# A Macaron transformer block on one core: the low halves of the expert weights are taken against a PSUM copy, the first shared results are summed by TensorE, and some table loads are issued later

## The chip, the cores and the metric

The kernel runs on one core of a Trainium2 chip. The metric is the device time of one execution in microseconds; the span of a profiled execution is the time from its first to its last instruction. TensorE is called PE here, its weight loads PEld, VectorE DVE, ScalarE ACT, GpSimd POOL and SyncE SP, as in the profile.

## What is computed

Two batches of 512 tokens with 256 features go through a mixture-of-experts layer, an attention layer and the same mixture-of-experts layer again, each added to the residual. The change lies in the first of the three.

```python
x = x + 0.5 * ffn(layernorm(x))          # 16 experts of width 128, 2 per token, and one shared expert
x = x + attention(layernorm(x))
x = x + 0.5 * ffn(layernorm(x))

def ffn(xt):
    probs = softmax(xt @ Wr.T + bias);  val, idx = top_k(probs, 2);  w = val / (val.sum() + 1e-9)
    y = (silu(xt @ Wg[e]) * (xt @ Wu[e])) @ Wd[e]          # for each expert e
    routed = sum over the two chosen experts of w * y
    shared = (silu(xt @ sWg) * (xt @ sWu)) @ sWd
    return routed + shared
```

## The kernel before

All products are taken in a three-term form: each fp32 operand is split into a high half that TensorE's one-pass format (`F32R`) holds exactly and a low half, the remainder, and `three` sums high times high, high times low and low times high. So each expert's weights, 768 words on each of 128 partitions, need a split: ACT copies `w_raw` to `wh` in the format of the high half (`split_high`, L656), and DVE subtracts `wh` from `w_raw` to get `wl` (`split_low`, L1230). `wl` lies on the memory of `w_raw`. Expert number q in the order of use is `order[q]`; q = 0 is the shared expert, 1 to 16 are the routed ones.

The engines run their own instruction lists in the order written and meet at semaphores; there is no scheduler. The first `ffn` has these stages:

- **Routing** (`route`): DVE works out for each token its two experts and the row (`slot`) of a table `slots_x` in DRAM that the token goes to. POOL then writes the normalised tokens there by 16 indirect DMAs (`scatter`, L565).
- **The shared expert** over eight tiles of 128 tokens, as a pipeline of turns i. In turn i PE runs `gate_up` of tile i (six matmuls of 256 columns), `hidden_turn` of tile i-1 (a transpose by the identity) and `down` of tile i-2 (three matmuls); ACT takes the silu of tile i (`sg`, L675), the high half of the hidden tile i-1 (`hT_h`, L681) and `split_high(8 + i)`; DVE multiplies (`hm`, L1330), takes the low half of the hidden tile (`hT_l`, L1334), adds half of the result of tile i-3 to the residual `res` (L1347) and runs `split_low`: one expert a turn up to turn 5, two a turn in turns 6 to 10.
- **The routed blocks**: 31 blocks of 128 rows of `slots_x`, loaded by SP as `xp` in pairs once all scatters have landed (L415), each through the same steps with the weights of its own expert. Before the first block PE waits for all low halves (`s_wlo_v`), for the residual sums (`s_ysh`), for the table of experts and for the scatters (`s_sc[3]`), and then runs six matmuls that only keep it busy (`keep_busy`, L877). The results go back to DRAM by one indirect DMA each (L576), from a ring of four buffers `ysb`.

SP loads the experts in order: ten together at the start, the last six in pairs, each pair behind a step of the scatters. Ahead of the ten, SP loads small tables for the attention mask (`place_k`, `place_q`, and `rows_k`, `rows_q` from `before` and `within`, which POOL fills). `s_place` counts POOL's four table steps.

## Time and profile before

| | us |
|---|---|
| median of three runs | 348.19 |
| lowest, highest | 347.44, 352.12 |
| the profiled execution | 348.41 |
| its span | 346.7 |
| shared expert, first matmul to the end of the last low half | 24.84 to 53.55 |
| first transpose of a routed block | 56.16 |

In the span PE is busy 74%, DVE 70%, ACT 48% and POOL 45% of the time. A row of the timeline gives the start in us, the duration in us, engine, line, operation and tiles, "x4" for four merged instructions, and in brackets the idle time before it and what ended that. A row of the chain of waits gives start, duration and the work. A row of the busy time by stretch gives the stretch, its length, the busy time of PE, PEld, DVE, ACT and POOL with their instructions, the granted PE clock as a share of 2.4 GHz, the share of the DMA engines and GB/s. A row of the groups gives line, engine, operation, tiles, shapes and count, then the busy time in all, the mean of one in ns, and the idle time before them.

### The profile page before, as it was taken

What the parts mean: (1) busy time and instruction counts of PE and PEld (TensorE: products, weight loads), DVE (VectorE), ACT (ScalarE), POOL (GpSimd) and SP (SyncE); (2) the same over time, 40 slices, a digit from 0 to 9 for tenths busy, and PEclk for the clock granted to TensorE, in tenths of its full rate; (3) what the DMA queues carried; (4) which work ended last, traced back from release to release, by engine and by line L of the source; (5) the groups of instructions that cost most, each with busy time, mean ns of one, the idle gap of its engine ahead of it and who ended that gap; (6) DMA issues with size and microseconds to landing.
All of it is one profiled execution on the core that took longest, in us unless ns stands there. A gap on an engine that the chain in (4) does not pass through costs nothing.

```text
span 346.7 us, 6303 instructions
## 1 busy us (share of the span) xinstructions
PE 255.0 (74%) x1812; PEld 185.4 (53%) x1815; DVE 243.5 (70%) x800; ACT 167.0 (48%) x433; POOL 155.6 (45%) x248
## 2 busy tenths in 40 slices
PE   1828537999991677987998999889459069999900
PEld 0528515999980255543343444457248039999800
DVE  8787593788876971758888889457586018888726
ACT  3486531555553155457656667773423015565400
POOL 7207770466766003303768733320027704776620
PEclk9967855999996899999999999999969769999955
DMA  7996919154512517991543300000002261456137
GB/s 252 407 363 207 352 66 298 45 149 122 177 53 70 174 47 195 229 285 60 126 93 94 94 2 3 1 3 0 0 20 104 106 197 50 148 159 189 30 110 253
DMA packets 30472, 46.23 MB, mean 133 GB/s; under 512 B 5391, under 2 KB 23573, under 8 KB 30056
## 3 DMA queue, kind: packets, MB, share of 16 engines
q1 hardware_dynamic: 24776, 33.97, 31.5%
q0 software_dynamic: 5664, 11.87, 11.0%
q8 instruction: 16, 0.26, 0.3%
q14 instruction: 16, 0.13, 0.1%
HBM read 27.98 MB, written 20.61 MB: 140 GB/s over the span
## 4 chain that ended last, share of the span: by engine, by line
PE 44%; DVE 22%; DMA 11%; POOL 8%; ACT 7%; issue 5%; SPq 1%; another core or an unknown queue 1%; POOLq 0%; DVEq 0%; ACTq 0%
PE bank L314 21%; POOL slots_x L565 5%; PE bank L1073 5%; DVE bank L1458 5%; PE bank L968 4%; PE bank L1036 3%; PE bank L321 3%; DVE wl L1230 3%; DMA results<-ysb,xp 2%; DMA yg<-results 2%; DMA w_raw<-in_experts 2%; DVE res L1402 2%; PE bank L892 2%; ACT ct L841 2%; DMA slots_x<-xn,slot 2%
## 5 line engine op out<-in xcount | busy, mean ns | idle before, releaser
L576 POOL DMA_INDIRECT results<-ysb,xp x62 | 60.9, 983 | 51.3 <-issue 35.0
L1458 DVE CUSTOM_DVE_ANT_0 bank<-bank,dec 128x512 f32<-128x512 f32 (+3 forms) x128 | 59.5, 520 | 14.9 <-PE bank L1036 13.6
L841 ACT ACTIVATE ct<-bank 128x512 f32<-128x512 f32 (+1 forms) x96 | 44.4, 521 | 19.6 <-PE bank L1049 19.2
L565 POOL DMA_INDIRECT slots_x<-xn,slot x32 | 33.5, 1048 | 33.1 <-DVE slot L1307 23.8
L622 POOL TENSOR_SCALAR_AFFINE_SELECT ct<-ct 128x256 f32<-128x256 f32 x64 | 24.5, 407 | 39.9 <-ACT ct L841 39.9
L721 ACT ACTIVATE xT_h<-bank 128x256 fp32r<-128x256 f32 x62 | 23.8, 384 | 38.4 <-PE bank L968 36.8
L314 PE MATMUL bank<-wh,xT_h 128*128 x124 | 40.9, 329 | 1.4 <-DVE xT_l L1357 1.2
L1330 DVE TENSOR_TENSOR hm<-sg,bank 128x128 f32<-128x128 f32 x78 | 22.4, 287 | 23.9 <-ACT sg L675 23.9
L1357 DVE TENSOR_TENSOR xT_l<-bank,xT_h 128x256 fp32r<-128x256 f32 x62 | 26.2, 423 | 18.5 <-ACT xT_h L721 18.3
L675 ACT ACTIVATE sg<-bank 128x128 f32<-128x128 f32 x78 | 21.5, 276 | 36.1 <-PE bank L314 36.0
L1036 PE MATMUL bank<-stk_q,stk_k 96*128 96x512 bf16 (+3 forms) x128 | 33.9, 304 | 3.0 <-DMA stk_q<-parts_d 1.3
L314 PE MATMUL bank<-wh,xT_l 128*128 x124 | 35.3, 285 | 0.0
L314 PE MATMUL bank<-wl,xT_h 128*128 x124 | 35.3, 284 | 0.0
L314 PE MATMUL bank<-wh,hT_h 128*128 (+1 forms) x78 | 29.7, 381 | 2.7 <-DVE res L1347 2.1
L1049 PE MATMUL bank<-stk_k,stk_q 120*128 120x512 bf16 (+3 forms) x128 | 30.1, 300 | 1.3 <-DMA stk_k<-mT 0.8
L877 PE MATMUL bank<-below_b,ident_b 128*128 128x512 bf16 x35 | 12.7, 513 | 22.1 <-DMA slots_x<-xn,slot 10.1
L1369 DVE COPY ysb<-bank 128x256 f32<-128x256 f32 x62 | 25.7, 415 | 2.4 <-DMA results<-ysb,xp 1.3
L892 PE MATMUL bank<-ident,hm 128*128 128x128 f32 x78 | 22.4, 287 | 6.4 <-DVE hm L1330 6.3
L314 PEld LDWEIGHTS bank<-wh,xT_h 128*128 128x128 f32 x124 | 23.9, 193 | 3.2 <-issue 3.1
L968 PE MATMUL bank<-ident,xp 128*128 128x128 f32 x124 | 24.7, 286 | 0.4 <-issue 0.4
L596 POOL DMA_DIRECT2D stk_q<-parts_d x24 | 12.2, 515 | 27.8 <-DMA parts_d<-part 20.9
L1036 PEld LDWEIGHTS bank<-stk_q,stk_k 96*128 96x128 bf16 x128 | 10.7, 97 | 25.3 <-DVE mmax L1458 19.6
(188 smaller groups left out, 671.0 us busy)
## 6 DMA issues: line engine op xcount, KB each, us to landing
xp<-slots_x SPq DMA_DIRECT2D x30, 257.0 KB, 2.8
w_raw<-in_experts SPq DMA_DIRECT2D x17, 384.0 KB, 6.3
yg<-results SPq DMA_DIRECT2D x16, 256.0 KB, 4.6
slots_x<-zeros SPq DMA_DIRECT2D x2, 1285.0 KB, 11.4
parts_d<-part SPq DMA_DIRECT2D x6, 384.0 KB, 3.9
stk_k<-parts_d SPq DMA_DIRECT2D x8, 192.0 KB, 3.8
stk_q<-parts_d POOLq DMA_DIRECT2D x8, 192.0 KB, 4.6
slots_x<-zeros SPq DMA_DIRECT2D x1, 1413.5 KB, 7.3
```

Of the source, the lines that this page charges most:

```text
L314: mm = eng.matmul(to, xs(k, a), ws(k, b), start=i == 0, stop=i == len(terms) - 1)
L565: pool.indirect_dma_start(slots_x, where, xn[:, t, :], None)\
L576: pool.indirect_dma_start(results, where, ysb[c % RING][:], None, bounds_check=4 * N - 1, oob_is_err=False).then_inc(s_ys[c % RING], 16)
L622: pool.affine_select(out=pair, in_=pair, compare_op=ALU.is_ge, fill=0.0, base=0, pattern=[[0, 2], [1, P]], channel_multiplier=-1).then_inc ...
L841: act.activation(ct[n % 6][:, a:b], bank[2 + i][:, 0:b - a], ACT.Exp).then_inc(s_exp, 1)
L892: pe.transpose(bank[4 + par][:, 0:P], hm[par][:], ident[:]).then_inc(s_ht, 1)
L968: mm = pe.transpose(bank[b % 2][:, k * P:(k + 1) * P], xb[b % XRING][:, k * P:(k + 1) * P], ident[:])
L1036: pe.matmul(bank[s_bank[num % 3]][:, 0:(i + 1) * P], stk_k[g % NSTK][0:STK, u, i * P:(i + 1) * P], stk_q[g % NSTK][0:STK, u, 0:(i + 1) * P ...
L1049: mm = pe.matmul(to[:, at:at + SEQ - j * P], q[:, u, j * P:(j + 1) * P], k[:, u, j * P:SEQ], start=at == 0, stop=True, skip_group_check=True)
L1357: dve.tensor_tensor(xT[b % 2][1][:], bank[b % 2][:, 0:D].rearrange("p (k t) -> p k t", k=KT), xT[b % 2][0][:].bitcast(F32), ALU.subtract). ...
L1369: dve.tensor_copy(ysb[r][:], bank[6 + (j - 3) % 2][:, 0:D]).then_inc(s_ye, 1)
L1458: dve.tensor_tensor_reduce(s_i, s_i, dec[:, SEQ - w:SEQ], 1.0, NEG, ALU.add, ALU.max, mmax[g % 2][:, n % G * QT + i:n % G * QT + i + 1])\
```

## The change

Four things are changed, all in the first `ffn` and ahead of it.

- `split_low_beside` takes the place of `split_low` for the 16 routed experts. PE multiplies the high half `wh` by an identity (`show_high`, two matmuls of 384 columns) into two PSUM banks, banks 6 and 7 for even q and 0 and 1 for odd q, and DVE subtracts these copies from `w_raw` in two instructions of 384 columns. `show_high(q)` waits for the high half and, since the banks are used again, for the low half of expert q-2.
- `down_and_add` takes the place of `down` for the shared tiles: PE adds twice the residual, by an fp32 matmul with a doubled identity, to the three products in PSUM banks 4 and 5, and ACT copies half of the sum to `res`. The addition on DVE is gone. Banks 4 and 5 also hold the transposed hidden tiles, so `hidden_turn` now waits for ACT's copy of the tile that was there.
- POOL fills the two identities (`ident_r`, `ident_2`) in the set-up. `iota_i` is made smaller.
- SP waits for two of POOL's table steps instead of four before the first mask tables, and loads `rows_k` and `rows_q` behind the first ten experts.

In PE's list, turn 3 of the shared expert (tile 3 enters, tile 2 is turned, tile 1 is brought down) ends like this before:

```order
L314 MATMUL bank<-wh,xnT_l 128x256
L892 MATMUL bank<-ident,hm 128x128 [waits s_htl,s_hm]
L314 MATMUL bank<-wh,hT_h 128x256 [waits s_htl]
L314 MATMUL bank<-wl,hT_h 128x256
L314 MATMUL bank<-wh,hT_l 128x256
L314 MATMUL bank<-wh,xnT_h 128x256 [waits s_hm]
```

and like this now, where L904 is the transpose, L914 and L916 are `down_and_add` and L958 is `show_high`:

```order
L319 MATMUL bank<-wh,xnT_l 128x256
L904 MATMUL bank<-ident,hm 128x128 [waits s_htl,s_hm,s_ysh]
L914 MATMUL bank<-res,ident 128x256 [waits s_htl]
L916 MATMUL bank<-wh,hT_h 128x256
L916 MATMUL bank<-wl,hT_h 128x256
L916 MATMUL bank<-wh,hT_l 128x256
L958 MATMUL bank<-wh,ident_r 128x384 [waits s_wlo_v,s_whi]
L958 MATMUL bank<-wh,ident_r 128x384
L319 MATMUL bank<-wh,xnT_h 128x256 [waits s_hm]
```

The transpose has a wait on ACT's copy (`s_ysh`) more, and the gate matmuls of the next tile stand behind two copies that wait for DVE (`s_wlo_v`).

In DVE's list, turn 8, where two experts are split and the last tiles come down, reads before:

```order
L1334 TENSOR_TENSOR hT_l<-bank,hT_h 128x128 [waits s_hth]
L1347 SCALAR_TENSOR_TENSOR res<-bank,res 128x256 [waits s_y]
L1230 TENSOR_TENSOR wl<-w_raw,wh 128x768 [waits s_whi] x2
```

and now, where L1282 is `split_low_beside` and L1387 the low half of the hidden tile:

```order
L1282 TENSOR_TENSOR wl<-w_raw,bank 128x384 [waits s_whp]
L1282 TENSOR_TENSOR wl<-w_raw,bank 128x384
L1282 TENSOR_TENSOR wl<-w_raw,bank 128x384 [waits s_whp]
L1282 TENSOR_TENSOR wl<-w_raw,bank 128x384
L1387 TENSOR_TENSOR hT_l<-bank,hT_h 128x128 [waits s_hth]
```

Each split now waits for PE's copy (`s_whp`), and the low half of the hidden tile has moved behind the splits of its turn.

The diff:

```diff
@@ -153,7 +153,9 @@
         oh = sb("oh", [P, 2, NT, E], F32, r2)
         ohs = sb("ohs", [P, NT, E], BF16, r2)
         big = sb("big", [P, NB * E], F32, r2)
-        iota_i = sb("iota_i", [P, 512], I32, r2)
+        iota_i = sb("iota_i", [P, 512 - 2 * P], I32, r2)
+        ident_r = sb("ident_r", [P, P], F32R, r2)
+        ident_2 = sb("ident_2", [P, P], F32, r2)
         mx = sb("mx", [P, NT], F32, r2)
         rsum = sb("rsum", [P, NT], F32, r2)
         top = sb("top", [P, 2, NT], F32, r2)
@@ -207,6 +209,7 @@
         s_w = [sem(f"s_w{q}") for q in range(E + 1)]
         s_whi = sem("s_whi")
         s_wlo_v = sem("s_wlo_v")
+        s_whp = sem("s_whp")
         s_rw = sem("s_rw")
         s_zero = sem("s_zero")
         s_eps = sem("s_eps")
@@ -295,6 +298,8 @@
 
         order = [E] + list(range(E))
         EARLY = 8
+        wh_bank = ((6, 7), (0, 1))
+        WP = WE // 2
         NJ = NT + NB
 
 
@@ -394,14 +399,15 @@
             sp.dma_start(ob[:], o_b.partition_broadcast(P)).then_inc(s_small, 16)
 
             at = SEQ + 1 + P
-            sp.wait_ge(s_place, 4)
+            sp.wait_ge(s_place, 2)
             for to in (place_k[0:3, :], place_q[5:8, :]):
                 sp.dma_start(to[0:2, :], masks[0:2, at:at + SEQ]).then_inc(s_msk, 16)
                 sp.dma_start(to[2:3, :], masks[6:7, at:at + SEQ]).then_inc(s_msk, 16)
+            for q in range(1, EARLY + 3):
+                load_expert(q)
+            sp.wait_ge(s_place, 4)
             sp.dma_start(rows_k[6:, :], before[:]).then_inc(s_msk, 16)
             sp.dma_start(rows_q[8:, :], within[:]).then_inc(s_msk, 16)
-            for q in range(1, EARLY + 3):
-                load_expert(q)
 
 
             for q, (gate_sem, count) in zip(range(EARLY + 3, E + 1, 2), ((s_to, 2), (s_sc[0], 8 * NT), (s_to, 3))):
@@ -534,6 +540,8 @@
             link(pool.memset(ones_b[:], 1.0))
             link(pool.affine_select(out=below_b[:], in_=ones_b[:], compare_op=ALU.is_gt, fill=0.0, base=0,
                                     pattern=[[1, P]], channel_multiplier=-1))
+            link(pool.tensor_copy(ident_r[:], ident[:]))
+            link(pool.tensor_scalar(ident_2[:], ident[:], 2.0, None, ALU.mult))
             pool.tensor_copy(ident_b[:], ident[:]).then_inc(s_const, 1)
             link(pool.memset(before[:], NEG))
             pool.affine_select(out=before[:], in_=before[:], compare_op=ALU.is_ge, fill=0.0, base=-1,
@@ -700,9 +708,13 @@
                 if f == 0:
                     for q in range(3, EARLY):
                         split_high(q)
-                for i in range(NT + 2):
+                for i in range(NT + 3):
                     if i < NT:
                         hidden(f * NJ + i, (f * NJ + i) % 2, i < 2 and not f)
+                    if f == 0 and 0 <= i - 3 < NT:
+                        act.wait_ge(s_y, i - 2)
+                        act.activation(res[:, i - 3, :], bank[4 + (i - 3) % 2][:, 0:D], ACT.Copy, scale=0.5)\
+                            .then_inc(s_ysh, 1)
                     if 0 <= i - 1 < NT:
                         hidden_high(f * NJ + i - 1, (f * NJ + i - 1) % 2, i - 1 < 2 and not f)
                     if f == 0 and EARLY + i <= E:
@@ -896,6 +908,14 @@
                 three(pe, bank[6 + par][:, 0:D], lambda k, a: hT[par][a][:], lambda k, b: wd(b),
                       [(0, 0, 0), (0, 0, 1), (0, 1, 0)]).then_inc(s_y, 1)
 
+            def down_and_add(t):
+                to = bank[4 + t % 2][:, 0:D]
+                pe.wait_ge(s_htl, t + 1)
+                pe.matmul(to, ident_2[:], res[:, t, :], start=True, stop=False)
+                for a, b in ((0, 0), (0, 1), (1, 0)):
+                    mm = pe.matmul(to, hT[t % 2][a][:], (wh, wl)[b][:, E, KT * GU:WE], start=False, stop=a == 1)
+                mm.then_inc(s_y, 1)
+
             def logits(n, r):
 
                 pe.wait_ge(s_tlo, number(n, r))
@@ -930,6 +950,19 @@
                     pe.wait_ge(s_wlo_v, 1)
                 pe.wait_ge(s_slot, 2 * f + 1)
 
+                def show_high(q):
+                    pe.wait_ge(s_whi, q + 1)
+                    if q > 2:
+                        pe.wait_ge(s_wlo_v, q - 1)
+                    for c in range(2):
+                        mm = pe.matmul(bank[wh_bank[q % 2][c]][:, 0:WP], ident_r[:],
+                                       wh[:, order[q], c * WP:(c + 1) * WP], start=True, stop=True,
+                                       skip_group_check=True)
+                    mm.then_inc(s_whp, 1)
+
+                if f == 0:
+                    show_high(1)
+
                 def w_s(k, b):
                     return (wh, wl)[b][:, E, k * GU:(k + 1) * GU]
 
@@ -938,11 +971,21 @@
                     if i < NT:
                         gate_up(j, j % 2, f == 0 and i < 2, rows(i), w_s)
                     if 0 <= i - 1 < NT:
+                        if f == 0 and i >= 3:
+                            pe.wait_ge(s_ysh, i - 2)
                         hidden_turn(j - 1, (j - 1) % 2, f == 0 and i - 1 < 2)
                     if 0 <= i - 2 < NT:
-                        if i - 2 >= 2:
+                        if f and i - 2 >= 2:
                             pe.wait_ge(s_ysh, f * NT + i - 3)
-                        down(j - 2, j % 2, lambda b: (wh, wl)[b][:, E, KT * GU:WE])
+                        if f == 0:
+                            down_and_add(i - 2)
+                        else:
+                            down(j - 2, j % 2, lambda b: (wh, wl)[b][:, E, KT * GU:WE])
+                    if f == 0:
+                        for q in (i + 2,) if i < 6 else (2 * i - 4, 2 * i - 3):
+                            show_high(q)
+                if f == 0:
+                    show_high(E)
                 pe.wait_ge(s_ysh, (f + 1) * NT)
                 if f == 0:
                     pe.wait_ge(s_wlo_v, E + 1)
@@ -1230,6 +1273,16 @@
                 dve.tensor_tensor(wl[:, e, :], w_raw[:, e, :], wh[:, e, :].bitcast(F32), ALU.subtract)\
                     .then_inc(s_wlo_v, 1)
 
+            def split_low_beside(q):
+                e = order[q]
+                for c in range(2):
+                    part = slice(c * WP, (c + 1) * WP)
+                    if c == 0:
+                        dve.wait_ge(s_whp, q)
+                    ins = dve.tensor_tensor(wl[:, e, part], w_raw[:, e, part], bank[wh_bank[q % 2][c]][:, 0:WP],
+                                            ALU.subtract)
+                ins.then_inc(s_wlo_v, 1)
+
             def statistics(r):
                 for t in (2 * r, 2 * r + 1):
                     ins = dve.bn_stats(stats[:, t, :], res[:, t, :])
@@ -1340,15 +1393,15 @@
                     j = f * NJ + i
                     if i < NT:
                         times_up(j, j % 2, f == 0 and i < 2)
+                    if f == 0:
+                        for q in (i + 1,) if i < 6 else (2 * i - 5, 2 * i - 4):
+                            split_low_beside(q)
                     if 0 <= i - 1 < NT:
                         hidden_low(j - 1, (j - 1) % 2)
-                    if 0 <= i - 3 < NT:
+                    if f and 0 <= i - 3 < NT:
                         dve.wait_ge(s_y, j - 2)
                         dve.scalar_tensor_tensor(out=res[:, i - 3, :], in0=bank[6 + (j - 3) % 2][:, 0:D], scalar=0.5,
                                                  in1=res[:, i - 3, :], op0=ALU.mult, op1=ALU.add).then_inc(s_ysh, 1)
-                    if f == 0:
-                        for q in (i + 1,) if i < 6 else (2 * i - 5, 2 * i - 4):
-                            split_low(q)
 
                 def step(b, live):
                     j = f * NJ + NT + b
```

## Rows read from the trace of the kernel before

**Rows 1.** Busy time by stretch, the shared expert.

```profile
24.80:30.70 5.90, 5.57 (x25) 5.30 (x26) 5.48 (x18) 5.68 (x12) 4.22 (x4) 0.50 0.79 306
...
40.90:44.35 3.45, 1.65 (x10) 1.05 (x9) 2.22 (x5) 2.97 (x7) 2.47 (x3) 0.99 0.63 244
44.35:53.65 9.30, 2.50 (x8) 1.64 (x8) 9.20 (x16) 2.04 (x4) 5.37 (x6) 0.50 0.31 97
```

**Rows 2.** The chain of waits in order of time, end of the shared expert.

```profile
45.08 0.33 DVE res L1347
...
51.81 1.75 DVE wl L1230 x2
...
53.65 2.72 PE bank L877 x6
```

**Rows 3.** Groups of DVE by shape, 18 to 112 us.

```profile
L1230 DVE TENSOR_TENSOR wl<-w_raw,wh 128x768 fp32r<-128x768 f32 x16 | 14.8, 947 | 0.0
L1357 DVE TENSOR_TENSOR xT_l<-bank,xT_h 128x256 fp32r<-128x256 f32 x31 | 13.1, 422 | 4.4 <-ACT xT_h L721 4.3
```

**Rows 4.** The timeline of PE, at half clock.

```profile
25.19 0.42 PE L314 MATMUL bank<-wl,xnT_h 128*128 128x256 f32 x1
25.41 0.41 PE L314 MATMUL bank<-wh,xnT_l 128*128 128x256 f32 x1
```

**Rows 5.** The same timeline, where the clock has risen.

```profile
30.44 0.39 PE L314 MATMUL bank<-wh,xnT_h 128*128 128x256 f32 x1
...
31.84 0.28 PE L314 MATMUL bank<-wl,xnT_h 128*128 128x256 f32 x1
31.96 0.28 PE L314 MATMUL bank<-wh,xnT_l 128*128 128x256 f32 x1
```

**Rows 6.** The same timeline in the attention: fp32 matmuls, four heads side by side.

```profile
166.47 1.07 PE L1073 MATMUL bank<-ct,V 128*32 128x512 f32 x8
...
169.55 0.64 PE L1073 MATMUL bank<-ct,V 128*32 128x256 f32 x8
```

**Rows 7.** The chain of waits among the blocks: two transposes.

```profile
71.69 0.22 PE bank L968 x2
```

**Rows 8.** The timeline of ACT, 35 to 42 us.

```profile
35.71 0.84 ACT L656 ACTIVATE wh<-w_raw 128x768 fp32r<-128x768 f32 x1 [3.81 <-DMA w_raw<-in_experts]
36.46 0.26 ACT L675 ACTIVATE sg<-bank 128x128 f32<-128x128 f32 x1
36.62 0.27 ACT L681 ACTIVATE hT_h<-bank 128x128 fp32r<-128x128 f32 x1
...
41.09 0.84 ACT L656 ACTIVATE wh<-w_raw 128x768 fp32r<-128x768 f32 x1 [3.13 <-DMA w_raw<-in_experts]
```

**Rows 9.** Groups of ACT by shape over the span.

```profile
L721 ACT ACTIVATE xT_h<-bank 128x256 fp32r<-128x256 f32 x62 | 23.8, 384 | 38.4 <-PE bank L968 36.8 <-issue 1.4
```

**Rows 10.** The timeline of POOL, set-up and scatters.

```profile
7.47 0.29 POOL L537 CAST ident_b<-ident 128x128 bf16<-128x128 f32 x1
...
13.21 0.19 POOL L557 COPY xn<-to_row 128x4 int32<-128x4 int32 x1 [2.23 <-DVE xn L1245]
...
43.03 1.62 POOL L565 DMA_INDIRECT slots_x<-xn,slot  x1 [0.52 <-POOL xn L557]
44.96 0.97 POOL L565 DMA_INDIRECT slots_x<-xn,slot  x1 [0.30 <-issue]
```

**Rows 11.** The timeline of SP's queue.

```profile
14.55 0.62 SPq L401 DMA_DIRECT2D rows_k<-before  x1
...
51.22 2.94 SPq L415 DMA_DIRECT2D xp<-slots_x  x6
```

**Rows 12.** DMA issues of the page, the blocks' loads: KB, us to landing.

```profile
xp<-slots_x SPq DMA_DIRECT2D x30, 257.0 KB, 2.8
```

**Rows 13.** Busy time by stretch: first transpose to first result, first and second expert layer.

```profile
56.16:63.21 7.05, 6.46 (x36) 5.99 (x35) 2.98 (x10) 2.79 (x10) 0.00 (x0) 0.63 0.62 214
...
282.22:287.85 5.63, 5.04 (x34) 4.26 (x35) 2.84 (x10) 2.54 (x9) 0.00 (x0) 0.91 0.62 195
```

## The prediction

> **What bounds the kernel now.** I read the chain of waits first, then the busy time by stretch, then the timelines of the engines in the first expert layer, since the diff touches nothing behind it. The chain shows that the shared expert ends on DVE: pairs of low halves of 1.73 to 1.75 us with a residual sum of 0.33 us between them, five times, up to 53.56; PE starts its six busy matmuls at 53.65 and the first block's transposes at 56.16 [rows 2, 13]. In that stretch PE is busy 2.50 of 9.30 us and DVE 9.20 [rows 1]. Two other things are close behind: ACT had waited 3.81 and 3.13 us for weights that landed at 35.71 and 41.09 [rows 8], and SP could load the blocks only from 51.22, when the last scatter had landed [rows 11]; a load lands 2.8 us after its issue [rows 12], so PE could not have begun a block before 54. The path that the change can shorten is thus worth about 2 us (56.16 to 54), plus what PE's clock gives: it is at 1.2 GHz from 44.35 on [rows 1], and from the first transpose to the first result the first layer takes 7.05 us at a mean clock of 0.63, the second layer, with the same work, 5.63 at 0.91 [rows 13].
>
> **The prices.** DVE: a low half of 768 columns takes 0.947, a subtraction of 256 columns with one operand in PSUM 0.422 [rows 3], that is 1.03 ns a column; so 384 columns take 0.55, and as the next may start 0.08 earlier (0.947 against half of 1.75), two hold DVE for 0.93, against 0.87 before. A PSUM operand costs nothing visible: the 256-column row lies on the same line. PE at 2.4 GHz: a matmul of 256 columns follows the last by 0.12 and ends 0.16 after that [rows 5]; at half clock by 0.21 to 0.22 [rows 4]. A copy (two of 384) is then 0.34, or 0.65 at half clock, and can be read 0.16 later, at 0.50. The fp32 matmul with the doubled identity has no twin in the trace. Below: two identity transposes of 128 columns take 0.22 [rows 7], above: the eight records of 256 columns of the attention take 0.64; I take the slope between its two rows, 1.07 less 0.64 for 256 columns more, 0.43 [rows 6], since that row, like this matmul, multiplies fp32 and doesn't only move it. The Trainium skill (FP8 and Floating Point Precision, section TensorE Precision Notes) says that a true fp32 product takes four passes through the array, which by the one-pass row would be an estimate of 0.47, far from the transposes' 0.22; with 0.22 the stage below ends 1.0 us earlier, and by the slope the trace agrees with the page. So the sum and product of one tile, `down_and_add`, is 0.43 + 3 x 0.12 = 0.79, against 0.36 before.
>
> **Part by part.** *Low halves beside a copy, and the residual on PE.* DVE alone would gain: in turns 6 to 10 ten splits cost 0.07 more each, five sums of 0.33 are gone, -0.95. But each turn of PE now has a ring of waits: gate matmuls until ACT can start its silu 0.95 (6 x 0.12, the tail, the semaphore), silu 0.16 [rows 8], ACT's copy of an earlier sum 0.42 (0.384 for 256 columns [rows 9] and the semaphore), for which the transpose waits, transpose 0.10, sum 0.79, copy 0.34, and only then the next gate matmuls: 2.76. The walk: PE is busy for 5.57 of the first 5.90 us at half clock [rows 1], so the three copies that stand ahead of the fourth gate group delay it by 3 x 0.65, from 30.44 [rows 5] to 32.4. From there the clock is full. Four turns of 2.76, 0.33 for the weights of 35.71, which ACT must still split ahead of a silu, and a second copy of 0.33 in turn 6 bring the gate matmuls of the last tile to 44.1. The weights of 41.09 are no longer waited for. The sum of tile 5 starts 1.63 later, at 45.7. Now PE and DVE hand over to each other: sum 0.79, copy 0.50, one split 0.93, low half of the hidden tile 0.33 (0.29 by the slope of rows 3, and the semaphore), then the next sum: 2.55, twice, to 50.8. The last time it is sum, copy, three splits and 0.16 to PE: 4.24. PE is let go at **55.1**, 1.4 us later than at 53.65. With the two bounds of the fp32 matmul it is 54.1 and 56.4.
>
> *Behind it.* If the clock is full there, the six busy matmuls take half of the 2.51 us from 53.65 to 56.16, 1.25: transposes at 56.3, +0.2. From there to the first result it is 5.63 instead of 7.05, -1.4. The sum is **-1.2 us**. After the first result the blocks run at full clock already, so the shift passes on to the end, through a list that isn't changed.
>
> *The scatters.* A scatter takes 0.97 when DVE reads PSUM or rests, and 1.62 where it starts beside low halves read from two SBUF operands [rows 10]; five of the 16 take 1.2 or more. The last scatter should land up to 2 us before 51.2, and the blocks be loaded before 52. With PE let go at 55.1 this is worth nothing; it is also why a scatter that isn't quickened costs nothing.
>
> *Tables later.* SP reaches the experts earlier by the two loads that now stand behind them, 0.62 us of issue for one [rows 11], and by the shorter wait. ACT may then split the first experts some 1.2 us earlier, but PE's first gate matmuls wait for DVE's routing, and the half-clock stretch above is PE's own: worth nothing to 0.3. `rows_k` and `rows_q` are read by ACT only after the last tile, long after they land. *POOL's two identities* take about 0.29 each like the cast beside them, and its next deadline, 13.21, has 2.23 us of idle time before it [rows 10]: nothing. *ACT's eight copies* of 0.38 lie in the ring, counted. Behind each waiting copy on PE stand the gate matmuls of the next tile, which ACT and DVE wait for; that is the ring too.
>
> **Rivals.** *The clock falls.* Between 40.90 and 44.35 PE was busy 1.65 of 3.45 us at full clock and fell to half at its end [rows 1]. In the ring it is busy 1.95 of 2.76 us (gate matmuls 0.72, transpose 0.10, sum 0.79, copy 0.34), but late, in the hand-over, 0.79 + 0.68 of 2.55, little more than the half of the stretch that fell. The Trainium skill (TensorE: Matmul & The Clock Gate, section What's actually happening) says that the throttled state is the default and activity releases it; by that rule more matmuls can only help, but the row at 40.90 shows a half-busy engine falling. If it falls near the end, the blocks start as cold as before: +1.4 from 55.1, 349.7. If a stretch of the ring runs at half clock as well, +1.1 on top and no gain behind it, 350.8; with all from 44 on at half clock PE is let go at 58.5, 353. This is the case that ends on the other side, decided by whether PE's gaps after 44 us pull the clock down. *The ring isn't there.* If the waits overlap better than I walked them, DVE sets the end as the change says: 53.65 less 0.95 is 52.7, busy matmuls at full clock to 53.95, blocks loaded by then: -2.2, and -1.4 behind: 344.8. For it: at full clock a copy of 0.50 fits into a split of 0.93. Against: the low half of the hidden tile now stands behind two splits, and the sum, and with it the copy, behind that. *Half clock throughout.* With the ring at 1.2 GHz the walk ends beyond 61, +8 or more, 356; PE would be busy nearly without a gap then, and in the first 5.90 us that raised the clock [rows 1]. *It does not do what it says*, scatters or loads keep their times: same time as the forecast, since neither is late.
>
> **How the numbers follow.** The profiled execution took 348.41, the median of the three is 348.19, 0.2 less; 348.41 less 1.2 is 347.2, from the median 347.0, and I say 347.1. Chances: forecast with the clock held 0.55 (346.0 to 348.5 with the bounds of the fp32 matmul), clock falls 0.23 (349.7 to 353), ring not there 0.18 (344.3 to 345.5), half clock throughout 0.04. The range takes in the forecast, half of the ring's absence and the falling clock up to one cold stretch: 344.6 to 351.0. Two per cent, about what a measurement of this kernel can tell from no change, is 7 us: only half clock throughout reaches it, and part of the falling clock could with bad luck; nothing here is worth 7 us of gain. Faster 0.01, same 0.94, slower 0.05.
>
> **What the profile after would show.** Right: DVE idle for some 0.5 us ahead of splits with PE's copy as releaser; PE waiting for ACT's `res` in turns 3 to 7; scatters all near 0.97; the six busy matmuls starting 1 to 2 us later than 53.65 with their waits last on DVE, and taking about 1.25 us. Wrong: DVE without gaps from 42 us on, a fp32 record pair away from 0.43, or a granted clock of 0.5 after 44 us.

## The result, and the profile after

The changed kernel takes 352.21 us (median of 20 runs, 348.25 to 356.85), the kernel before, timed beside it, 348.78 (345.01 to 352.12). The ratio is 1.0075, with a 95% interval of 1.0048 to 1.0102. That is 2.6 us by the ratio and 3.4 by the medians (the medians hold all runs, the ratio leaves out those more than 1.5% above the fastest): slower, though by less than 2%. The prediction was 347.1, with a range that ended at 351.0. The profiled execution took 352.48, with a span of 350.7.

PE's timeline in turn 6 of the shared expert and at the start of turn 7, after (start, duration, engine, line, work, and in brackets the idle time ahead and what ended it):

```profile
41.56 0.28 PE L319 MATMUL bank<-wh,xnT_h 128*128 128x256 f32 x1
...
43.07 0.33 PE L904 MATMUL bank<-ident,hm 128*128 128x128 f32 x1 [0.64 <-ACT res L716]
43.24 0.60 PE L914 MATMUL bank<-res,ident 128*128 128x256 f32 x2
...
44.03 0.87 PE L958 MATMUL bank<-wh,ident_r 128*128 128x384 f32 x4
44.73 0.29 PE L319 MATMUL bank<-wh,xnT_h 128*128 128x256 f32 x1
```

and ACT's in turn 6:

```profile
42.46 0.28 ACT L683 ACTIVATE sg<-bank 128x128 f32<-128x128 f32 x1 [0.83 <-PE bank L319]
42.64 0.38 ACT L716 ACTIVATE res<-bank 128x256 f32<-128x256 f32 x1
```

This is the ring, step by step: gate matmuls at 41.56, silu 0.90 later, ACT's copy 0.18 behind it, the transpose 0.43 behind that with `res` of ACT as its releaser, the sum from 43.24 to 44.03 (0.79), the copies of the high halves, and only then the next gate matmuls. A turn with one copy takes 2.82 us (33.11, 35.93, 38.75, 41.56). From 44 us on DVE waits for PE's copies:

```profile
44.58 1.02 DVE L1282 TENSOR_TENSOR wl<-w_raw,bank 128x384 fp32r<-128x384 f32 x2 [0.59 <-PE bank L958]
...
47.77 1.02 DVE L1282 TENSOR_TENSOR wl<-w_raw,bank 128x384 fp32r<-128x384 f32 x2 [0.59 <-PE bank L958]
...
53.19 2.88 DVE L1282 TENSOR_TENSOR wl<-w_raw,bank 128x384 fp32r<-128x384 f32 x6 [0.57 <-PE bank L958]
```

PE's end of the stage, after, and the busy time by stretch (columns as in [rows 1]):

```profile
54.36 0.59 PE L958 MATMUL bank<-wh,ident_r 128*128 128x384 f32 x2 [0.85 <-DVE wl L1282]
56.17 1.76 PE L889 MATMUL bank<-below_b,ident_b 128*128 128x512 bf16 x6 [1.22 <-issue]
57.72 0.63 PE L1011 MATMUL bank<-ident,xp 128*128 128x128 f32 x2
```

```profile
24.80:30.70 5.90, 4.82 (x21) 4.71 (x22) 5.07 (x19) 4.87 (x10) 3.22 (x3) 0.57 0.71 272
44.35:53.65 9.30, 6.80 (x39) 5.41 (x37) 7.19 (x17) 4.14 (x12) 2.98 (x5) 1.00 0.54 163
...
57.72:65.17 7.45, 6.86 (x36) 6.46 (x35) 2.90 (x10) 2.78 (x10) 0.00 (x0) 0.58 0.10 38
```

In the stretch 44.35 to 53.65, at a granted clock of 0.50 before [rows 1], the clock is 1.00. PE is let go at 56.17, where it was 53.65 before [rows 2]. The six busy matmuls take 1.55 to the first transpose instead of 2.51, but then the clock falls: from the first transpose to the first result it is 7.45 us at a mean clock of 0.58, where 5.63 was expected [rows 13].

The scatters did what the prediction said: all but the first take 0.96 to 0.98, where 1.62 stood before [rows 10], and SP loads the blocks from 49.08 instead of 51.22 [rows 11]. PE doesn't wait for that.

```profile
46.56 0.96 POOL L573 DMA_INDIRECT slots_x<-xn,slot  x1 [0.30 <-issue]
```

```profile
49.08 2.94 SPq L421 DMA_DIRECT2D xp<-slots_x  x6
```

In these two profiles the first layer accounts for 1.3 us (last result of a block copied at 106.39, before at 105.09), and 2.8 are lost behind it, in code that the change doesn't touch. Whether that second part belongs to the change was the first thing to settle.

### The profile page after: what moved, and what is told of

Read it like the earlier page. It is cut to its first block, busy times and chain, and to the rows that moved or that the text cites. A ratio compares the mean times of both kernels' runs of the same rounds, so it can differ in the third digit from the quotient of the medians.

```text
span 350.7 us, 6428 instructions
## 1 busy us (share of the span) xinstructions
PE 265.0 (76%) x1863; PEld 194.6 (55%) x1863; DVE 243.0 (69%) x808; ACT 170.7 (49%) x441; POOL 153.2 (44%) x250
## 4 chain that ended last, share of the span: by engine, by line
PE 43%; DVE 19%; POOL 10%; DMA 10%; issue 10%; ACT 7%; SPq 1%; POOLq 0%; DVEq 0%
PE bank L319 17%; PE bank L1116 5%; DVE bank L1511 5%; POOL slots_x L573 4%; DMA results<-ysb,xp 4%; PE bank L326 3%; PE bank L1079 3%; POOL results L584 3%; PE bank L1011 3%; DMA yg<-results 2%; ACT ct L853 2%; PE bank L904 2%; DVE res L1455 2%; PE bank L1092 2%; PE bank L958 2%
## 5 line engine op out<-in xcount | busy, mean ns | idle before, releaser
L573 POOL DMA_INDIRECT slots_x<-xn,slot x32 | 31.4, 982 | 33.5 <-DVE slot L1360 24.5
L319 PE MATMUL bank<-wh,xT_h 128*128 x124 | 41.9, 338 | 2.0 <-DVE xT_l L1410 2.0
L319 PEld LDWEIGHTS bank<-wh,xT_h 128*128 128x128 f32 x124 | 24.9, 201 | 3.4 <-issue 3.3
L319 PE MATMUL bank<-wh,hT_h 128*128 (+1 forms) x70 | 25.7, 367 | 0.9 <-DVE hT_l L1387 0.4
L904 PE MATMUL bank<-ident,hm 128*128 128x128 f32 x78 | 22.2, 285 | 4.0 <-ACT res L716 3.2
L319 PEld LDWEIGHTS bank<-wl,xT_h 128*128 128x128 f32 x124 | 25.1, 202 | 0.0
L319 PEld LDWEIGHTS bank<-wh,xT_l 128*128 128x128 f32 x124 | 24.8, 200 | 0.0
```

The costliest lines, as they stand in the source:

```text
L319: mm = eng.matmul(to, xs(k, a), ws(k, b), start=i == 0, stop=i == len(terms) - 1)
L573: pool.indirect_dma_start(slots_x, where, xn[:, t, :], None)\
L904: pe.transpose(bank[4 + par][:, 0:P], hm[par][:], ident[:]).then_inc(s_ht, 1)
```

## Experiments

The theories. **The ring** (of waits on PE, with ACT's copy in it) lets PE go late. **The cold tail**: the clock falls while PE waits from 53 to 56, and the blocks start at half clock. **The set-up**: POOL's two identities delay the routing. **Luck**: what is lost behind the first layer is a matter of single executions. The medians and ratios, each against the kernel before timed beside it (20 runs of the changed kernel, 6 of ident_act, 12 of each other):

| kernel | median | before | ratio, 95% |
|---|---|---|---|
| changed | 352.21 | 348.78 | 1.0075 (1.0048 to 1.0102) |
| copy_first | 349.88 | 347.78 | 1.0059 (1.0026 to 1.0092) |
| no_copies | 351.15 | 347.78 | 1.0091 (1.0055 to 1.0128) |
| no_sum | 350.61 | 347.78 | 1.0060 (1.0026 to 1.0094) |
| ident_act | 354.27 | 347.78 | 1.0107 (1.0024 to 1.0189) |
| setup_only | 348.69 | 348.41 | 1.0030 (0.9991 to 1.0070) |
| before_busy | 347.62 | 348.41 | 0.9991 (0.9946 to 1.0036) |
| after_busy | 350.21 | 348.41 | 1.0059 (1.0024 to 1.0095) |
| best1 | 347.16 | 348.41 | 0.9980 (0.9942 to 1.0018) |
| before_fill | 347.05 | 348.89 | 0.9941 (0.9911 to 0.9971) |
| after_fill | 351.33 | 348.89 | 1.0051 (1.0014 to 1.0087) |
| before_all | 345.03 | 348.89 | 0.9880 (0.9843 to 0.9917) |
| best2 | 345.91 | 348.89 | 0.9946 (0.9906 to 0.9986) |

### The ring: copy_first

```diff
                 for i in range(NT + 3):
-                    if i < NT: hidden(...)
                     if f == 0 and 0 <= i - 3 < NT: ... res[:, i - 3, :] copied
+                    if i < NT: hidden(...)
```

> The changed kernel, with ACT's residual copy of a turn ahead of its silu instead of behind it. If the ring of waits sets the end of the shared expert, a turn of PE in turns 4 to 7 falls from 2.82 to about 2.4 us, PE no longer waits 0.64 us for ACT's res, and the six busy matmuls start at about 54.9 instead of 56.17; the last result scatter of the first layer then comes about 1.2 us earlier and the median falls by as much, 0.3%. If DVE's splits alone set the end, the busy matmuls still start at 56.0 to 56.3 and the time stays. If the cold start behind it is what costs, the block transposes come earlier but the gate matmuls behind them still run at half clock, and the time stays above that of before by 0.3% or more.

PE's timeline of this kernel in turn 7, and its end of the stage:

```profile
44.11 0.27 PE L904 MATMUL bank<-ident,hm 128*128 128x128 f32 x1
44.22 0.60 PE L914 MATMUL bank<-res,ident 128*128 128x256 f32 x2
...
54.14 2.60 PE L889 MATMUL bank<-below_b,ident_b 128*128 128x512 bf16 x6 [1.23 <-issue]
```

The wait for `res` is gone ahead of the transpose (but for turn 4, where weights that landed at 35.95 held ACT); a turn with one copy takes 1.96 (38.43 to 40.39), and PE is let go at 54.14, 2.0 us earlier. So in these executions the ring set the end. By the medians of all runs 2.3 us come back, by the ratios (1.0059 and 1.0075) only 0.6, and their intervals can't tell this kernel from the changed one.

### The halves of the change: no_copies and no_sum

no_copies takes `show_high` out of PE's list and puts before's `split_low` back, behind the low half of the hidden tile; no_sum keeps the copies and lets DVE add the residual:

```diff
-                        if f == 0:
-                            down_and_add(i - 2)
+                        down(..., 6 if f else 4)          # banks 4 and 5 in the first layer
...
+                    if f == 0 and 0 <= i - 3 < NT:      # DVE, first in its turn
+                        dve.wait_ge(s_y, j - 2)
+                        dve.scalar_tensor_tensor(out=res[:, i - 3, :], in0=bank[4 + (j - 3) % 2][:, 0:D], ...)
```

> The changed kernel without PE's copies of the high halves: DVE splits as before from two SBUF operands, behind the low half of the hidden tile; TensorE's sum with the residual and ACT's copy stay. By the walk with the measured durations the last split ends at 52.1 and only the loads of the blocks hold PE, until about 54; POOL's scatters take 1.6 again. By the theory that the copies are what makes PE late: time 2 us below the changed kernel, at or below before. By the rival that TensorE's sum is what makes it late: the same time as the changed kernel, busy matmuls at 56.

> The changed kernel without TensorE's sum: the three products still go to banks 4 and 5, DVE adds half of them to the residual first in its turn, and ACT copies nothing. PE's copies of the high halves stay. By the walk the busy matmuls start at about 54.5, 1.6 us before the changed kernel. By the theory that the hand-over of copies and splits between PE and DVE sets the end, at 56 as in the changed kernel. Scatters stay at 0.97 in both.

Neither came out as expected: by the ratios each half alone costs as much as both. PE's timeline of no_copies, one turn and the end:

```profile
44.73 0.48 PE L904 MATMUL bank<-ident,hm 128*128 128x128 f32 x1 [0.64 <-ACT res L716]
45.00 1.06 PE L914 MATMUL bank<-res,ident 128*128 128x256 f32 x2
...
48.62 0.48 PE L904 MATMUL bank<-ident,hm 128*128 128x128 f32 x1 [0.64 <-ACT res L716]
...
57.49 2.72 PE L889 MATMUL bank<-below_b,ident_b 128*128 128x512 bf16 x6 [3.82 <-issue]
```

The ring is still there, and PE, without the copies, runs at half clock in this execution (0.52 from 40 to 53): the turn takes 3.89 instead of 2.82, and PE is let go at 57.49. In no_sum the place of ACT's copy is taken by DVE's sum, which stands behind two splits:

```profile
49.24 0.33 PE L900 MATMUL bank<-ident,hm 128*128 128x128 f32 x1 [0.78 <-DVE res L1389]
...
51.60 0.39 PE L319 MATMUL bank<-wh,hT_h 128*128 128x256 f32 x1 [0.75 <-DVE hT_l L1380]
...
56.02 1.85 PE L885 MATMUL bank<-below_b,ident_b 128*128 128x512 bf16 x6 [1.55 <-issue]
```

PE and DVE wait for each other, and PE is let go at 56.02. What both halves share is the waiting step that was put between a tile's product and the next transpose (banks 4 and 5 are now used for both). That this step is the price of each half is argued from these rows and not shown: the two profiled executions took 356.16 and 354.67 us, 4 to 5 above the medians of their kernels, and in both a late expert held ACT (landed at 39.50 and 37.28, after waits of 1.34 and 2.39).

### The set-up: ident_act and setup_only

ident_act makes the identities on ACT, in the idle time between two of its copies; setup_only gives the kernel before the changed POOL list and SP order and nothing else.

```diff
-            link(pool.tensor_copy(ident_r[:], ident[:]))
-            link(pool.tensor_scalar(ident_2[:], ident[:], 2.0, None, ALU.mult))
...
+                if r == 4:
+                    act.wait_ge(s_const, 1)
+                    act.activation(ident_r[:], ident[:], ACT.Copy)
+                    act.activation(ident_2[:], ident[:], ACT.Copy, scale=2.0)
```

> The changed kernel, with the two identities made by ACT in a gap of its own instead of by POOL ahead of the mask tables. If POOL's 1.1 us of added work holds up DVE's normalisation, DVE's split of the router weights takes 0.17 again instead of 0.61, the third pair of transposes starts at 11.6 instead of 12.13, and the first matmul of the shared expert comes 0.5 to 1.05 us before 25.89; of the end that is worth 0.1 (if the weights that land at 36 hold the shared expert anyway) to 1.0 us. If POOL has nothing to do with it, the first matmul stays at 25.8 to 26.0.

> The kernel before, with only the changed kernel's set-up: POOL also fills the two identities (nobody reads them), and SP waits for two table steps and loads two tables behind the first ten experts. If POOL's work is what delays the routing, the first matmul of the shared expert comes 0.5 to 1.05 us after 24.84 and the median rises by 0.1 to 0.3%. If all that the four variants so far share costs more than that, by clock falls behind the first layer, the ratio comes out near 1.006 as theirs. If the set-up is free, 24.8 and a ratio of 1.000.

DVE's split of the router weights and PE's first matmul of the shared expert, in the changed kernel:

```profile
9.41 0.61 DVE L1464 TENSOR_TENSOR rw_l<-rw_s,rw_h 128x32 fp32r<-128x32 f32 x1
```

```profile
25.89 0.98 PE L958 MATMUL bank<-wh,ident_r 128*128 128x384 f32 x2 [2.21 <-issue]
```

and in ident_act:

```profile
9.56 0.17 DVE L1466 TENSOR_TENSOR rw_l<-rw_s,rw_h 128x32 fp32r<-128x32 f32 x1
```

```profile
25.31 0.98 PE L960 MATMUL bank<-wh,ident_r 128*128 128x384 f32 x2 [2.21 <-issue]
```

So POOL's identities do delay the routing, by 0.58 us here, and setup_only has its first matmul at 25.93 instead of 24.84. All profiles agree: the ten with the identities on POOL have it at 25.49 to 25.93, the ten without at 24.32 to 25.36. But the end does not follow: PE is let go at 56.11 in ident_act (56.17 with the identities on POOL) and at 53.05 in setup_only, whose ratio has 1.000 in its interval. In both, ACT still waits for weights that land at 35.5 to 35.8 us. The interval of setup_only reaches 1.0070, though, so its runs alone don't rule a cost out. The 1.0107 of ident_act has only six runs behind it and the widest interval of all; it doesn't say that ACT's identities cost anything.

### The cold tail: after_busy, before_busy and a mended kernel

after_busy and before_busy add matmuls that only keep PE busy, where it waits; best1 has copy_first, ident_act, 11 such matmuls, and the low half of the hidden tile between the two splits of a turn.

```diff
 # after_busy: 3 and 4 ahead of the last two down_and_add, and
                 if f == 0:
+                    keep_busy(bank[3], 4)
                     show_high(E)
+                    keep_busy(bank[3], 5)
 # before_busy
+                if f == 0:
+                    keep_busy(bank[5], 14)
                 pe.wait_ge(s_ysh, (f + 1) * NT)
 # best1, in DVE's turn
+                    if f == 0 and i >= 6: split_low_beside(2 * i - 5)
                     if 0 <= i - 1 < NT: hidden_low(j - 1, (j - 1) % 2)
+                    if f == 0: split_low_beside(i + 1 if i < 6 else 2 * i - 4)
```

> The kernel before, with 14 more matmuls that only keep TensorE busy, ahead of its last waits of the shared expert (they fill the idle 48.5 to 53.65). Price of the cold start of the blocks: if it is the 1.4 us that the prediction took, plus 1.2 for the six busy matmuls at full clock, the first result scatter comes 2.6 us earlier and the ratio is 0.993. If loads of the blocks (at 54) hold PE then, 1.4 to 2.2 us, ratio 0.995. If the clock falls again behind the blocks' start, or does not rise, 1.000.

> The changed kernel, with 16 matmuls that only keep TensorE busy in the gaps of its last three turns (2 to 4 each, 9 behind the last sum). If the idle tail from 53.2 to 56.2 is what lets the clock fall, the clock stays at 1.0 from 44 to 61, the six busy matmuls take 1.3 instead of 1.8 and the transposes of the first block start at 57.4, the first result scatter comes about 1.7 us earlier: 350.5 where the changed kernel has 352.2, ratio to the kernel before 1.002 to 1.004. If the cold start has another reason, the ratio stays at 1.0075 or rises, since the matmuls can only be in the way.

> The changed kernel with all mends at once: identities by ACT, ACT's residual copy ahead of the silu, the low half of the hidden tile between the two splits of a turn, and 11 keep-busy matmuls in the last gaps. By the ring, the set-up and the cold tail the sum against the changed kernel is 0.1 to 0.6, 2.2 and 1.7: busy matmuls at 53.5 to 54, transposes at 55, first layer 4 us earlier than the changed one: ratio to the kernel before 0.992 to 0.996. If half or more of the difference lies behind the first layer whatever is done in it (copying first gave 2 us back there and the ratio stayed at 1.006), 1.000 to 1.004.

PE's timeline of before_busy, and of best1, at the end of the stage:

```profile
46.58 4.79 PE L877 MATMUL bank<-below_b,ident_b 128*128 128x512 bf16 x14
52.02 1.45 PE L877 MATMUL bank<-below_b,ident_b 128*128 128x512 bf16 x6 [0.65 <-issue]
53.31 0.60 PE L970 MATMUL bank<-ident,xp 128*128 128x128 f32 x4
```

```profile
51.29 2.85 PE L891 MATMUL bank<-below_b,ident_b 128*128 128x512 bf16 x11
53.97 0.60 PE L1017 MATMUL bank<-ident,xp 128*128 128x128 f32 x4
```

In these two and in after_busy the clock is at 1.0 from 55 to 100, and in before_busy the first result of a block is copied at 58.63, 4.5 us earlier than in the profile of the kernel before (63.13). Yet the median of before_busy gains only 0.8. after_busy has its first transposes at 59.48 and not at 57.4: the clock was at 1.0 from 44 to 61 as expected, but in this execution it was at 0.69 from 30 to 38, and the gate matmuls of the fourth tile came at 35.10 instead of 33.11. best1's median is 3.1 us below that of after_busy, and its ratio lies 0.95%, 3.3 us, below that of the changed kernel (0.998 and 1.0075, intervals apart), so the mends together work; it equals the kernel before within its interval.

### Behind the first layer: four kernels with more busy matmuls

```diff
+            keep_busy(bank[5], 30)
             pe.wait_ge(s_yg[0], 16)
-            keep_busy(bank[5], 7)
+            keep_busy(bank[5], 22)
...
+                if f:
+                    keep_busy(bank[5], 44)
                 pe.wait_ge(s_bex, f + 1)
```

These go into the kernel before (before_fill), the changed kernel (after_fill), before_busy (before_all) and best1 (best2).

> The kernel before, with keep-busy matmuls in TensorE's two longest waits behind the first expert layer: 30 ahead of the attention, 15 and 6 more in its first gaps, and 44 ahead of the blocks of the second layer. The first layer is as before (last result scatter at 106 to 107). If the clock in these places is what spreads the time behind the first layer, the second layer's six busy matmuls take 1.3 instead of 2.7 and its blocks start at full clock, the first projections too: 2 to 3 us less than before, ratio 0.992 to 0.995, and a smaller spread. If the falls come elsewhere whatever TensorE does here, 1.000.

> The changed kernel with the same matmuls behind its first layer, which is left as it is. If the 2.6 us that the changed kernel lost are 1.3 in the first layer and clock falls behind it, it comes out 1.0 to 1.6 us above the kernel before with these matmuls, 0.3 to 0.45% (ratio to before 0.996 to 0.999). If the change itself costs something behind the first layer, the distance between the two stays at 0.75%.

> The kernel before with the 14 keep-busy matmuls ahead of its first blocks and the same ones as above behind the first layer. The 14 alone brought the last result scatter of the first layer from 107.3 to 102.0, and the median 0 to 1 us. If falls of the clock in the gaps behind took the rest, 5 us below the kernel before with the later matmuls alone: ratio to before 0.978 to 0.985. If the chip takes back what was granted, wherever it was granted, 0.995 to 1.000.

> The mended changed kernel with the later matmuls. Its first layer ended at 102.5. By the theory of the falls in the gaps: 4 to 5 us below the kernel before with the later matmuls alone, as the kernel before with all keep-busy matmuls, ratio 0.980 to 0.987. By the theory of the grant that is taken back: 0.995 to 1.000.

The busy time by stretch from 100 to 125 us, in before_busy:

```profile
100.00:125.00 25.00, 13.85 (x45) 7.11 (x46) 19.06 (x55) 7.44 (x15) 4.33 (x4) 0.66 0.26 85
```

and in before_fill, with the start of the second layer's blocks (there 282.76 is the first transpose):

```profile
100.00:125.00 25.00, 22.27 (x109) 12.01 (x109) 20.04 (x58) 7.37 (x18) 7.37 (x7) 1.00 0.28 86
282.76:288.39 5.63, 4.83 (x37) 4.36 (x38) 2.99 (x10) 2.66 (x10) 0.00 (x0) 1.00 0.60 195
```

The clock holds there, and there is a gain against the kernel before: 1.8 us in before_fill and 3.9 in before_all. The latter's ratio, 0.988, lies between the two forecasts, so neither theory about what is granted is shown; best2 with 0.9946 gained less than the first of them. The theory of luck fails, though: after_fill and before_fill stand 4.3 us apart by the medians and 1.1% by the ratios, where 1.0 to 1.6 us was expected. Holding the clock behind the first layer doesn't bring the two kernels closer.

### Where the loss is: kernels that end behind the first layer

Attention and second layer are left out, and the residual behind the first layer is stored (`return` behind `ffn(0)` on each engine).

> The kernel before, ended behind the first expert layer: attention and second layer are left out and the residual behind the first layer is the output. About 107.3 for the last scatter plus the combination and the stores, some 125 us.

> The changed kernel, ended in the same place. If all of the loss is made in the first layer, it is 2.6 to 3.6 us above before_first; if the layer loses what the profiles show, 1.3 to 2.0 us; what is missing then is lost behind it.

> The changed kernel with ACT's residual copy ahead of the silu, ended in the same place. By the ring: 1.2 to 2.0 us below after_first, near before_first. If the ring costs nothing since the blocks start cold all the same: as after_first.

> The changed kernel with 16 keep-busy matmuls in the gaps of its last turns, ended in the same place. If the cold start costs what the prediction took, 1.4 to 2 us below after_first; if the matmuls only stand in the way, 0.3 to 0.6 above it (its profile had the transposes at 59.5, 1.8 later, and the last result scatter 0.5 earlier).

| kernel | median, us | runs |
|---|---|---|
| before_first | 120.84 | 5 |
| after_first | 124.26 | 4 |
| copy_first_first | 121.86 | 4 |
| after_busy_first | 123.70 | 4 |

The difference of 3.4 us is there whole (after_first at 123.08 to 124.89, four of the five runs of before_first at 119.59 to 120.96): all of the loss is made in the first layer, and without the ring 2.4 us of it go. The busy matmuls give 0.6, less than expected and within the spread of four runs; in the profile of after_first the blocks were at full clock without them. before_first itself came out 4 us under its 125, with the last result scatter at 102.66 in its profile and not at 107.26. Why the profiles showed only 1.3 is seen where PE is let go in before_first, and in what ACT waited for ahead of it:

```profile
38.63 0.85 ACT L654 ACTIVATE wh<-w_raw 128x768 fp32r<-128x768 f32 x1 [0.95 <-DMA w_raw<-in_experts]
```

```profile
51.19 2.72 PE L876 MATMUL bank<-below_b,ident_b 128*128 128x512 bf16 x6 [4.91 <-DVE wl L1230]
53.81 0.67 PE L967 MATMUL bank<-ident,xp 128*128 128x128 f32 x4
```

and in after_first:

```profile
56.18 1.46 PE L888 MATMUL bank<-below_b,ident_b 128*128 128x512 bf16 x6 [1.22 <-issue]
57.47 0.60 PE L1010 MATMUL bank<-ident,xp 128*128 128x128 f32 x4
```

In the kernel before the end hangs on the landing of the late experts. The one that landed at 41.09 in the profile before [rows 8] landed at 38.63 here, and both times PE is let go 12.56 us later, at 53.65 and 51.19. In setup_only and before_fill it was the expert ahead of it that held ACT a turn earlier:

```profile
38.86 0.84 ACT L661 ACTIVATE wh<-w_raw 128x768 fp32r<-128x768 f32 x1 [1.93 <-DMA w_raw<-in_experts]
53.05 2.72 PE L882 MATMUL bank<-below_b,ident_b 128*128 128x512 bf16 x6 [5.16 <-DVE wl L1235]
```

```profile
38.95 0.84 ACT L656 ACTIVATE wh<-w_raw 128x768 fp32r<-128x768 f32 x1 [3.20 <-DMA w_raw<-in_experts]
53.13 2.72 PE L877 MATMUL bank<-below_b,ident_b 128*128 128x512 bf16 x6 [5.12 <-DVE wl L1233]
```

These are four executions of the same shared expert (setup_only's behind the changed set-up), with a mean of 52.8: the profile that the prediction started from was the latest of them. In the changed kernel the ring sets the end, and a late landing moves it less. In after_fill an expert held ACT for 1.63 us, and PE is let go 0.53 later than in the profile after:

```profile
36.63 0.84 ACT L664 ACTIVATE wh<-w_raw 128x768 fp32r<-128x768 f32 x1 [1.63 <-DMA w_raw<-in_experts]
56.70 2.72 PE L889 MATMUL bank<-below_b,ident_b 128*128 128x512 bf16 x6 [1.23 <-issue]
```

PE is let go 3.6 us later in the mean, but that is not yet the loss: the same executions stand closer together behind it (us from the start of the span).

| execution | PE let go | first result copied | last result copied |
|---|---|---|---|
| before | 53.65 | 63.13 | 105.09 |
| before_first | 51.19 | 59.20 | 100.48 |
| setup_only | 53.05 | 62.63 | 103.73 |
| before_fill | 53.13 | 62.72 | 104.05 |
| mean | 52.76 | 61.92 | 103.34 |
| changed | 56.17 | 65.17 | 106.39 |
| after_first | 56.18 | 62.89 | 104.50 |
| after_fill | 56.70 | 64.89 | 106.12 |
| mean | 56.35 | 64.32 | 105.67 |

The changed kernel makes 1.2 of the 3.6 us good up to the first result, and at the last one it is 2.3 behind, near the 2.6 by the ratio. The 3.4 between the medians is more than that; with single executions as far apart as 100.48 and 105.09 the rest can't be assigned.

The last two kernels compare the mended change with the kernel before when both hold the clock:

> The kernel before with 14 keep-busy matmuls ahead of its first blocks, ended behind the first layer. If the cold start of the blocks is worth what its traces show (six busy matmuls 1.3 instead of 2.7, first results 1.4 us earlier), 118 to 118.8, where before_first took 120.84. If half the executions start warm anyway, 120.

> The mended changed kernel (ACT's copy first, low half of the hidden tile between the splits, identities by ACT, 11 keep-busy matmuls), ended behind the first layer. Its last split ended at 52.6 and that of the kernel before with keep-busy matmuls at 51.9 to 52.6. If the copies on TensorE, once mended, gain what DVE saves, it is 0.5 us or more below before_busy_first; if the weights' landing or the loads of the blocks at 54 set the start, the two are within 0.5 us; if the rest of the ring still costs, 0.5 to 1 us above.

119.92 us (117.46 to 122.20) and 120.30 (118.67 to 121.71), six runs each: the spread is wider than the differences that were asked about, so whether the mended change gains or loses here stays open. The median of before_busy_first also missed its 118 to 118.8, though two of its runs lie at 117.46 and 118.79. A likely reason, not tested, is that the cold start that it removes is not there in every execution (the first result came 5.4 us after the first transpose in before_first, 7.0 in the profile before).

## Why the prediction was wrong

**The walk through the ring held in its steps.** A turn was to take 2.76 and took 2.82; ACT's wait, the transpose's wait on `res`, the sum of 0.79 and the 0.43 of the fp32 product are as worked out. PE was to be let go at 55.1, with bounds of 54.1 and 56.4, and it was at 56.17, or 56.35 in the mean of three: 0.7 of the difference is there at the gate matmuls of the fourth tile (33.11 for 32.4), the rest is 0.1 to 0.2 in each hand-over of the end. That the ring makes PE late is shown by copy_first (54.14, and 2.4 us less where the kernels end behind the first layer). The rival that the ring isn't there is refuted.

What failed is the sum: +1.4 us until PE is let go and -2.7 from there to the first result were to make -1.2. By the means above it is +3.6 and -1.2, so +2.4. Of the 3.6 us between the two sums 0.9 lie in the point of comparison, 1.2 in the length of the walk, inside its own bounds, and 1.5 in the gain behind it.

**The first step that failed is the point of comparison**: "PE is let go at 55.1, 1.4 us later than at 53.65". The 53.65 was one execution, held up by an expert that landed at 41.09. The prediction had the row of that wait [rows 8] and used it for a cause that the change would remove, but didn't ask whether the kernel before would meet it in its other executions. Against the mean of four, 52.8, the walk's own 55.1 would have been +2.3.

**The second, and the larger one, is the gain behind it**: "it is 5.63 instead of 7.05, -1.4" and a further 1.3 of 2.51 on the six busy matmuls. The clock was at 1.00 until 53.65, as forecast, but PE then waits for DVE's last three splits, and what follows differs from execution to execution: the six busy matmuls of the changed shared expert take 1.76, 1.46 and 2.72 in three profiles, and from the first transpose to the first result it is 7.45, 5.42 and 5.67. The kernel before gets the short way in one of its four (5.4 in before_first, 7.0 to 7.1 in the others). So the gain is there in some executions, 1.2 us in the mean, and no 2.7 can be booked; what decides between the two ways is not shown. That was the rival of the falling clock, with its 349.7 to 353 and a chance of 0.23; the time came out in it, though more than half of the miss lies in the other two terms.

**The set-up** was put at "nothing", with 0.29 us for each identity. At its place that was wrong: they took 0.29 and 0.62, and the routing came 0.58 later, most of it by a split that took 0.61 instead of 0.17. At the end the let-go times of ident_act and setup_only show no cost. **The tables** moved behind the experts cost or gave nothing that setup_only could show. **The scatters** were right, and PE did not wait for them, as said.

What stays open is how much of the loss beside the ring's part belongs to the hand-over of the end and how much to the clock: the 0.6 of after_busy_first, from four runs, can't tell. It is open too why taking the ring's wait out gives 2.4 us where the kernels end behind the first layer and only 0.6 by the ratios of the whole kernels. The kernel that beats both is the one before with more busy matmuls, before_all, by 1.2%; the mended change with the same matmuls, best2, by 0.5%; six runs of the two with the first layer alone don't tell them apart.

## What to carry to other kernels

A stage that ends on the engine with most work doesn't get shorter by taking work off that engine if the work comes back as a wait in another engine's list: write down the ring of waits for one turn, with its steps, and compare it with the busy time that was the bound. Compare a walk with several executions of the place where the kernel before ends, above all where a load that lands at changing times sets it; one profile can be a microsecond off. The work that was moved to TensorE held its clock here, but what counted was the clock after the next wait, and matmuls that do nothing, added to the kernel before, held that at less cost.

## What the runs showed of the hardware

In these traces a POOL operation that starts first holds a DVE operation up. In the changed kernel POOL's selection into `before` started at 9.37 and DVE's split of 32 columns at 9.41, and the split took 0.61, to the end of POOL's; in ident_act the split started at 9.56, as did POOL's next selection, and took 0.17. It is 0.60 or 0.61 in the ten profiles with the identities on POOL, 0.17 or 0.18 in the ten others. The Trainium skill (SBUF — State Buffer, section SBUF: two separate sides) says that the port that the two share is an exclusive lock for a whole instruction, held by whichever starts first, and that a DVE operation with two SBUF inputs contends with a POOL operation that reads SBUF. By that rule it is the start, 0.04 us apart, that decides; the trace of the changed kernel agrees, while in ident_act the two starts can't be told apart. The scatters show a like effect from the other side: 0.96 to 0.98 beside splits with an operand in PSUM, up to 1.62 and more beside splits with two in SBUF [rows 10]. no_copies, which brings the two SBUF operands back, has one of 1.73 again:

```profile
46.68 1.73 POOL L573 DMA_INDIRECT slots_x<-xn,slot  x1 [0.30 <-issue]
```

The same six matmuls behind the same wait took 1.46, 1.76 and 2.72 us in three executions. The Trainium skill (TensorE: Matmul & The Clock Gate, section What's actually happening) says that the window in which the chip judges TensorE's activity runs freely and isn't reset when a kernel starts; three executions that differ fit that, and show no more. And where the copies of the high halves were taken away, the other matmuls were slower: in the one execution of no_copies that was profiled the records of an fp32 sum went from 0.60 to 1.06 us, at a granted clock of 0.52 from 40 to 53 us.
